# A two-stage convolution block: each engine's program as one free sequence over the images instead of a repeated period

## The chip, the cores and the metric

The kernel runs on one core of a Trainium2 chip. The metric is the device time of one execution in microseconds (us), less is better. Five engines each work through their own queue in order: TensorE (PE in the profile), VectorE (DVE), ScalarE (ACT), GpSimd (POOL) and SyncE (SP), which here only issues DMA transfers. They meet through semaphores.

## The reference

The input x is 8 images of 32 channels, 64 x 64, float32. Two residual blocks follow each other, each behind a group norm with one group per channel:

```python
x = x + L0_conv_ref(gn(x), gate, value, geom, pw weights)   # adaptive 3x3 kernel, R = 4 kernels per pixel
x = x + L1_conv_ref(gn(x), w1, w2, w3)                      # three 3x3 convolutions, 32-64-64-32

# inside L0: per pixel, from 1x1 products of the normed x
mu   = softmax(gate)                                        # 4 weights
kern = exp(-(pu / sig_u) ** 2 - (ps / sig_s) ** 2)          # 4 x 9 taps, from theta, base, hyper
w    = mu * kern; w = w / (sum(w) + 1e-6)
agg  = einsum('brsl,bcsl->brcl', w, patches of the value)   # 4 x 32 channels
out  = einsum('bkhw,ok->bohw', agg, pw_w) + pw_b
```

L1 is three plain 3x3 convolutions in a row.

## The kernel before, in words

**Front of an image (L0).** An image lies in SBUF as 4 quarters of 16 rows by 32 channels on 128 partitions. `gn1_stats`, `gn1_sums`, `gn1_spread`, `gn1_scale`, `gn1_rstd`, `gn1_bias` pass the statistics over VectorE, TensorE and GpSimd; `norm1` (ScalarE) writes the normed xc. `geometry` (L386) makes the gate and geometry values of all pixels, and the eight parts of `tap_weights` on VectorE and six on ScalarE turn them into five tap weights per pixel: the centre and four pairs, since opposite taps have the same weight. `v_product` (L395) and `v_evict` make the value image vn, `halo` copies its border rows between quarters by DMA, and `pair_sum` (L1019, GpSimd) adds opposite neighbours. For each of 10 units u (two halves h of five taps) `values` (L412) transposes the value onto pixels, and `mult` (L712, VectorE, 2,048 elements per partition) multiplies it with the weights. `add_products` (L1003 on GpSimd, L722 on VectorE) adds the five products of a half; in image 0 three of the four adds of a half are done by TensorE in the transposes. `transpose_sums` (L427) transposes back, `sums_out` copies to SBUF, `pointwise` (L440) is the 1x1 product, `residual` (L741) adds x and the bias into x2.

**Between.** The second norm (`gn2_...`, `norm2`) writes y, which is split into a high and a low part (`split_high` on ScalarE L924, `split_low` on VectorE L755). `by_slots` (L287) moves both by DMA into the layout of the convolutions, four groups of 4 high and 4 low transfers each. `by_quads` (L296) moves x2 to x2r, for the last add.

**Convolutions (L1).** Eleven chunks of output rows: four of layer 1, five of layer 2, two of layer 3. A term (`conv_term`, L366) is three matmuls, high by high, low by high, high by low weight. There are 60 terms per image: chunks of layer 1 have 3 each, of layer 2 6, of layer 3 9. `high_part` (ScalarE L929) rounds a chunk, `take_high` (L380) subtracts it in PSUM, `low_part` (ScalarE L937, for the last image VectorE L730) copies the rest. Two PSUM banks alternate, so a chunk starts only when the chunk two before it has its low part out. `result` (L763, VectorE) adds the last two chunks to x2r, and `store` writes them.

**Order.** Every engine has a `body(i)`, a list of steps with image offsets written out by hand; `run_images` calls it for i from -4 to 12, and `on` drops steps of images that don't exist:

```python
def on(i, step, *args):
    if 0 <= i < IMAGES:
        step(i, *args)
...
convs(i - 3, 57, 58)
on(i - 1, transpose_sums, 1)
```

So each engine repeats one period per image. TensorE has the convolutions of image i - 2 between the front steps of images i - 1 and i. In the first periods the conv steps are empty, in the last ones the front steps are.

Of the kernel before, what the change touches and what calls it, by code (L numbers as in the profile page):

```python
# [26 lines left out]
FIRST, LAST = -4, IMAGES + 5  # L27
# [35 lines left out]


def conv_l0_l1_kernel(nc, x, geo_w, geo_bias, val_w, pw_t, pw_b, w1, w2, w3, ident, sel_quarter,
                      masks, consts, out):
    ctx = ExitStack()
    with ctx:
# [110 lines left out]

        def on(i, step, *args):  # L180
            if 0 <= i < IMAGES:
                step(i, *args)

        def run_images(body):
            for i in range(FIRST, LAST):
                body(i)
# [61 lines left out]
        def _(sp):  # L248
# [56 lines left out]
            def body(i):  # L305
                on(i - 1, by_slots, 0, False)
                on(i - 1, by_slots, 1, False)
                on(i - 1, by_slots, 0, True)
                on(i - 1, by_slots, 1, True)
                on(i - 1, by_slots, 2, False)  # L310
                on(i - 1, by_slots, 2, True)
                on(i - 1, by_slots, 3, False)
                on(i - 1, by_slots, 3, True)
                on(i + 1, halo)
                on(i - 2, store)
                on(i - 1, by_quads)
                on(i + 2, load_x)

            run_images(body)
# [21 lines left out]
        def _(pe):  # L341
# [127 lines left out]
            def convs(i, first, end):  # L469
                for k in range(first, end):  # L470
                    on(i, conv_term, k)

            def body(i):
                convs(i - 3, 41, 42)
                on(i - 1, values, 4)
                convs(i - 3, 42, 46)
                on(i - 1, values, 5)
                on(i, geometry)
                convs(i - 3, 46, 48)
                on(i - 3, take_high, 8)  # L480
                convs(i - 3, 48, 50)
                on(i, v_product, 0)
                convs(i - 3, 50, 51)
                on(i - 1, values, 6)
                on(i - 1, values, 7)
                convs(i - 3, 51, 55)
                on(i, v_product, 1)
                convs(i - 3, 55, 57)
                on(i - 1, transpose_sums, 0)
                convs(i - 3, 57, 58)  # L490
                on(i - 1, transpose_sums, 1)
                on(i - 1, transpose_sums, 2)
                convs(i - 3, 58, 60)
                convs(i - 2, 0, 3)
                on(i - 1, transpose_sums, 3)
                on(i - 1, values, 8)
                convs(i - 2, 3, 4)
                on(i - 2, take_high, 0)
                convs(i - 2, 4, 6)
                on(i - 1, values, 9)  # L500
                convs(i - 2, 6, 7)
                on(i - 2, take_high, 1)
                convs(i - 2, 7, 12)
                on(i - 2, take_high, 2)
                on(i - 1, pointwise, 0)
                convs(i - 2, 12, 13)
                on(i - 2, take_high, 3)
                convs(i - 2, 13, 18)
                on(i - 1, transpose_sums, 4)
                on(i - 1, transpose_sums, 5)  # L510
                convs(i - 2, 18, 19)
                on(i - 1, transpose_sums, 6)
                on(i - 2, take_high, 4)
                on(i - 1, transpose_sums, 7)
                convs(i - 2, 19, 20)
                on(i, values, 0)
                convs(i - 2, 20, 21)
                on(i - 1, pointwise, 1)
                convs(i - 2, 21, 26)
                on(i, values, 1)  # L520
                convs(i - 2, 26, 27)
                on(i - 1, gn2_sums, 0)
                convs(i - 2, 27, 29)
                on(i - 1, gn2_sums, 1)
                on(i - 2, take_high, 5)
                on(i, values, 2)
                convs(i - 2, 29, 30)
                on(i + 1, gn1_sums, 0)
                convs(i - 2, 30, 31)
                on(i - 2, take_high, 6)  # L530
                on(i + 1, gn1_sums, 1)
                convs(i - 2, 31, 40)
                on(i - 2, take_high, 7)
                on(i, values, 3)
                convs(i - 2, 40, 41)

            run_images(body)

        @block.vector
        def _(dve):  # L540
# [225 lines left out]
            def body(i):  # L766
                on(i - 4, mult, 7)
                on(i - 4, mult, 8)
                on(i - 4, add_products, 1, 1)
                on(i - 4, mult, 9)  # L770
                on(i - 5, low_part, 0)
                on(i - 4, add_products, 1, 2)
                on(i - 3, tap_weights, 4)
                on(i - 4, add_products, 1, 3)
                on(i - 3, tap_weights, 5)
                on(i - 4, residual, 0)
                on(i - 3, split_weights)
                on(i - 3, tap_weights, 6)
                on(i - 3, tap_weights, 7)
                on(i - 4, residual, 1)  # L780
                on(i - 4, gn2_stats, 0)
                on(i - 5, low_part, 1)
                on(i - 4, gn2_stats, 1)
                on(i - 3, mult, 0)
                on(i - 4, gn2_spread)
                on(i - 2, gn1_stats)
                on(i - 4, gn2_scale)
                on(i - 2, gn1_spread)
                on(i - 5, low_part, 2)
# [38 lines left out]
        def _(act):  # L828
# [111 lines left out]
            def body(i):  # L940
# [163 lines left out]
```

## Time and profile before

| | us |
|---|---|
| median of 3 runs | 549.23 |
| lowest, highest | 548.38, 549.37 |
| the profiled execution | 549.03 |
| its span | 547.2 |
| TensorE busy (mean granted clock 0.973) | 483.3 |
| VectorE busy | 419.4 |
| ScalarE busy | 216.3 |
| GpSimd busy | 191.4 |

Times inside the span count from its start. The span is what the profiler saw of the engines; the execution is 1.8 us longer. "Busy" of TensorE counts a matmul from its start to its modelled end, and matmuls overlap, so a busy share of 100% does not say that each matmul takes its shortest time. The granted clock is a share of the full TensorE clock: 1.00 is 2.4 GHz, 0.50 is 1.2 GHz. A line such as "[2.67 <-DVE prod L722]" says that the engine had been idle for 2.67 us and that the event which ended it came from VectorE's instruction of line 722.

### The profile page before, as it was taken

What the parts mean: (1) busy time and instruction counts of PE and PEld (TensorE: products, weight loads), DVE (VectorE), ACT (ScalarE), POOL (GpSimd) and SP (SyncE); (2) the same over time, 40 slices, a digit from 0 to 9 for tenths busy, and PEclk for the clock granted to TensorE, in tenths of its full rate; (3) what the DMA queues carried; (4) which work ended last, traced back from release to release, by engine and by line L of the source; (5) the groups of instructions that cost most, each with busy time, mean ns of one, the idle gap of its engine ahead of it and who ended that gap; (6) DMA issues with size and microseconds to landing.
All of it is one profiled execution on the core that took longest, in us unless ns stands there. A gap on an engine that the chain in (4) does not pass through costs nothing.

```text
span 547.2 us, 7160 instructions
## 1 busy us (share of the span) xinstructions
PE 483.3 (88%) x2527; PEld 391.8 (72%) x2527; DVE 419.4 (77%) x553; ACT 216.3 (40%) x408; POOL 191.4 (35%) x95
## 2 busy tenths in 40 slices
PE   2505973789999999999999999999999999998995
PEld 2204752566887788777977797779777987886894
DVE  2598678999898989898989989998989698412211
ACT  1520631265335543643355344644364313340110
POOL 1305524572366117520934083506370542000000
PEclk9999995589999999999999999999999999999999
DMA  4100002430144113421233124321431144024302
GB/s 145 42 1 0 5 0 56 98 72 17 46 97 100 40 38 87 93 59 44 69 95 69 47 53 107 65 55 41 100 77 25 36 95 86 22 56 107 70 5 38
DMA packets 40275, 32.23 MB, mean 59 GB/s; under 512 B 26160, under 2 KB 30768, under 8 KB 40240
## 3 DMA queue, kind: packets, MB, share of 16 engines
q1 hardware_dynamic: 40240, 31.78, 25.1%
q8 instruction: 20, 0.33, 0.3%
q14 instruction: 15, 0.12, 0.1%
HBM read 5.66 MB, written 4.19 MB: 18 GB/s over the span
## 4 chain that ended last, share of the span: by engine, by line
PE 64%; DVE 16%; issue 9%; SPq 4%; ACT 2%; POOL 1%; DMA 1%; DVEq 0%; ACTq 0%; POOLq 0%
PE conv_ps L366 42%; PE agg_ps L427 7%; DVE prod L712 6%; DVE prod L722 5%; PE val_ps L412 5%; SPq L287 4%; PE geo_ps L395 3%; PE geo_ps L386 3%; PE pw_ps L440 2%; PE conv_ps L380 2%; DMA xraw<-in_x 1%; POOL prod L1003 1%; DVE st L546 1%; DVE trig L643 1%; POOL vs L1019 1%
## 5 line engine op out<-in xcount | busy, mean ns | idle before, releaser
L712 DVE TENSOR_TENSOR prod<-val_ps,tapw 128x2048 f32<-128x2048 f32 x80 | 181.0, 2284 | 11.6 <-PE val_ps L412 10.2
L366 PE MATMUL conv_ps<-c_hi,wc_hi 128*128 128x448 f32 (+2 forms) x384 | 157.1, 409 | 0.0
L366 PE MATMUL conv_ps<-c_hi,wc_lo 128*128 128x448 f32 (+2 forms) x384 | 144.6, 376 | 0.0
L366 PE MATMUL conv_ps<-c_lo,wc_hi 128*128 128x448 f32 (+2 forms) x384 | 144.1, 375 | 0.0
L1003 POOL TENSOR_TENSOR prod<-prod 128x2048 f32<-128x2048 f32 x23 | 112.5, 4894 | 16.4 <-DVE prod L712 16.4
L1019 POOL TENSOR_TENSOR vs<-vn 128x1024 f32<-128x1024 f32 x32 | 69.6, 2185 | 74.2 <-ACT vn L843 73.4
L722 DVE TENSOR_TENSOR prod<-prod 128x2048 f32<-128x2048 f32 x35 | 88.7, 2533 | 1.0 <-POOL prod L1003 0.5
L366 PEld LDWEIGHTS conv_ps<-c_hi,wc_hi 128*128 128x128 f32 x384 | 72.5, 189 | 21.7 <-issue 8.3
L366 PEld LDWEIGHTS conv_ps<-c_hi,wc_lo 128*128 128x128 f32 x384 | 72.3, 188 | 10.6
L366 PEld LDWEIGHTS conv_ps<-c_lo,wc_hi 128*128 128x128 f32 x384 | 72.7, 189 | 9.7 <-issue 2.4
L929 ACT ACTIVATE c_hi<-conv_ps 128x512 fp32r<-128x512 f32 (+4 forms) x88 | 41.9, 485 | 86.4 <-PE conv_ps L366 86.2
L412 PE MATMUL val_ps<-ident_sb,vs 128*128 128x128 f32 x256 | 42.3, 300 | 24.0 <-DVE prod L712 22.2
L937 ACT ACTIVATE c_lo<-conv_ps 128x512 fp32r<-128x512 f32 (+4 forms) x77 | 36.3, 481 | 68.1 <-PE conv_ps L380 67.8
L993 POOL TENSOR_TENSOR gn<-gn 128x1 f32<-128x1 f32 x8 | 4.4, 552 | 167.7 <-DVE gn L560 167.7
L412 PEld LDWEIGHTS val_ps<-ident_sb,vs 128*128 128x128 f32 x256 | 34.4, 155 | 32.2 <-DVE prod L712 23.6
L427 PE MATMUL agg_ps<-ident_sb,prod 128*128 128x128 f32 x352 | 47.0, 278 | 7.6 <-DVE prod L722 5.9
L427 PEld LDWEIGHTS agg_ps<-ident_sb,prod 128*128 128x128 f32 x352 | 41.5, 144 | 16.6 <-issue 9.9
L908 ACT ACTIVATE agg<-agg_ps 128x512 f32<-128x512 f32 x64 | 36.5, 593 | 25.5 <-PE agg_ps L427 25.4
L366 PE MATMUL conv_ps<-xq_hi,wc_hi 128*128 128x512 f32 x96 | 40.1, 418 | 1.6 <-DMA xq_lo<-y_lo 1.6
L763 DVE TENSOR_TENSOR x2r<-conv_ps,x2r 128x512 f32<-128x512 f32 x16 | 11.0, 688 | 36.1 <-PE conv_ps L366 36.1
L366 PE MATMUL conv_ps<-xq_lo,wc_hi 128*128 128x512 f32 x96 | 38.6, 402 | 0.0
L366 PE MATMUL conv_ps<-xq_hi,wc_lo 128*128 128x512 f32 x96 | 38.4, 400 | 0.0
(107 smaller groups left out, 506.6 us busy)
## 6 DMA issues: line engine op xcount, KB each, us to landing
xq_hi<-y_hi SPq DMA_DIRECT2D x128, 66.0 KB, 2.0
xq_lo<-y_lo SPq DMA_DIRECT2D x128, 66.0 KB, 2.0
xraw<-in_x SPq DMA_DIRECT2D x32, 128.0 KB, 2.8
x2r<-x SPq DMA_DIRECT2D x128, 32.0 KB, 1.9
out_y<-x2r SPq DMA_DIRECT2D x32, 128.0 KB, 2.8
prod<-in_w SPq DMA_DIRECT2D x1, 576.0 KB, 4.8
vn<-vn SPq DMA_DIRECT2D x16, 24.8 KB, 1.8
prod<-in_w SPq DMA_DIRECT2D x1, 384.0 KB, 3.9
```

Of the source, the lines that this page charges most:

```text
L287: sp.dma_start(dst[C * s:C * s + C, j0:j0 + K8, :].bitcast(F32), src[C * g:C * g + C, (s + 1) % 2, :, :].bitcast(F32)).then_inc(xq_in[g], 16)
L366: mm = nc.tensor.matmul(bank[:, 0:conv_cols(n)], weights, lo if part == 1 else hi, start=term == part == 0, stop=final and part == 2)
L386: mm = nc.tensor.matmul(geo_ps[:, k * GEO:(k + 1) * GEO], xc[:, k * P:(k + 1) * P], geo_w_sb[:, :], start=k == 0, stop=k == K8 - 1, skip_g ...
L412: mm = nc.tensor.matmul(val_ps[u % 2][:, kk * P:(kk + 1) * P], src, ident_sb[:, :], is_transpose=True, start=kk == 0, stop=kk == KK - 1, s ...
L427: mm = nc.tensor.matmul(agg_ps[n % 2][:, kk * P:(kk + 1) * P], product(i, TAPS * h + b)[:, at0:at0 + P], ident_sb[:, :], is_transpose=True ...
L712: v.tensor_tensor(dst, val.unsqueeze(2).to_broadcast([P, B, R, C]), wgt.unsqueeze(3).to_broadcast([P, B, R, C]), ALU.mult).then_inc(mult_d ...
L722: v.tensor_tensor(product(i, TAPS * h + a), product(i, TAPS * h + a), product(i, TAPS * h + b), ALU.add).then_inc(add_v, 1)
L908: s.activation(agg[:, n % G, :], agg_ps[n % 2][:, :], ACT.Copy).then_inc(agg_sb, 1)
L929: op = s.activation(hi, src, ACT.Copy)
L937: op = s.activation(lo, src, ACT.Copy)
L1003: p.tensor_tensor(product(i, TAPS * h + a), product(i, TAPS * h + a), product(i, TAPS * h + b), ALU.add).then_inc(add_g, 1)
L1019: p.tensor_tensor(vs[:, n], vn[:, a[0], a[1]], vn[:, b[0], b[1]], ALU.add).then_inc(pairs_done, 1)
```

## The change

`on`, `run_images` and the five `body` functions go. In their place each engine has a flat list of calls, one per step and image. The steps' own code, their waits, buffers and engines are unchanged, and each engine issues the same instructions. Only their order in each queue is new, and it is no longer the same for every image. From the diff (removed lines are all of this kind: `on(i - 3, mult, 1)`):

```diff
-FIRST, LAST = -4, IMAGES + 5
-        def run_images(body):
-            for i in range(FIRST, LAST):
-                body(i)
@@ SyncE
-            def body(i): ...
+            load_x(0); load_x(1); halo(0); halo(1); load_x(2)
+            by_slots(0, 0, False) ... by_slots(0, 3, True)
+            halo(2); by_quads(0); load_x(3)
...
+            by_slots(2, 2, True); halo(4); by_slots(2, 3, False); by_slots(2, 3, True)
+            store(1); by_quads(2); load_x(5)
...
+            store(4); halo(7); by_quads(5)
@@ TensorE
+            gn1_sums(0, 0); gn1_sums(0, 1); geometry(0); v_product(0, 0); v_product(0, 1)
+            gn1_sums(1, 0); gn1_sums(1, 1)
+            values(0, 0) ... values(0, 4); geometry(1); values(0, 5)
+            transpose_sums(0, 0); transpose_sums(0, 1); values(0, 6); transpose_sums(0, 2)
+            values(0, 7); v_product(1, 0); transpose_sums(0, 3); v_product(1, 1)
+            values(0, 8); values(0, 9); values(1, 0); pointwise(0, 0)
+            transpose_sums(0, 4) ... transpose_sums(0, 7); pointwise(0, 1)
+            gn2_sums(0, 0); values(1, 1); gn2_sums(0, 1); gn1_sums(2, 0)
+            values(1, 2); values(1, 3); gn1_sums(2, 1); values(1, 4); values(1, 5)
+            geometry(2); values(1, 6); values(1, 7); convs(0, 0, 1); v_product(2, 0)
+            convs(0, 1, 3); v_product(2, 1); convs(0, 3, 6); transpose_sums(1, 0)
...
+            convs(0, 53, 60); transpose_sums(2, 0); transpose_sums(2, 1); convs(1, 0, 1)
...
+            convs(1, 53, 60); convs(2, 0, 1); transpose_sums(3, 0)
...
+            convs(2, 55, 57); transpose_sums(4, 0)        # then (5, 0) behind convs(3, 56, 58),
+            # (6, 0) behind convs(5, 0, 2), (7, 0) behind convs(5, 49, 58)
...
+            pointwise(7, 1); convs(6, 22, 26); gn2_sums(7, 0); convs(6, 26, 27)
+            take_high(6, 5); gn2_sums(7, 1); convs(6, 27, 34) ... convs(7, 0, 60)
@@ VectorE
+            gn1_stats(0); gn1_spread(0); gn1_scale(0); gn1_bias(0)
+            tap_weights(0, 0); tap_weights(0, 1); split_weights(0)
+            tap_weights(0, 2); tap_weights(0, 3); gn1_stats(1); tap_weights(0, 4); tap_weights(0, 5)
+            gn1_spread(1); tap_weights(0, 6); gn1_scale(1); tap_weights(0, 7); gn1_bias(1)
+            mult(0, 0) ... mult(0, 4); tap_weights(1, 0); tap_weights(1, 1); mult(0, 5)
+            tap_weights(1, 2); mult(0, 6); tap_weights(1, 3); mult(0, 7); mult(0, 8); mult(0, 9)
+            residual(0, 0); tap_weights(1, 4); gn2_stats(0, 0); tap_weights(1, 5); tap_weights(1, 6)
+            residual(0, 1); gn2_stats(0, 1); gn2_spread(0); tap_weights(1, 7); gn2_scale(0)
+            mult(1, 0); gn1_stats(2); gn2_bias(0); gn1_spread(2); mult(1, 1); mult(1, 2); mult(1, 3)
+            gn1_scale(2); split_low(0); gn1_bias(2); mult(1, 4); mult(1, 5)
...
+            mult(3, 5); tap_weights(4, 2); result(1, 0); add_products(3, 0, 3)
+            tap_weights(4, 3); mult(3, 6); result(1, 1)
...
+            tap_weights(7, 2); result(4, 0); add_products(6, 0, 3); tap_weights(7, 3); result(4, 1)
@@ ScalarE
+            norm1(0); split_weights(0); tap_weights(0, 0); v_evict(0, 0)
...
+            high_part(6, 5); low_part(6, 5); norm2(7); split_high(7); high_part(6, 6)
@@ GpSimd
+            gn1_rstd(0); pair_sum(0, 0); pair_sum(0, 1); gn1_rstd(1); pair_sum(0, 2); pair_sum(0, 3)
+            add_products(0, 0, 0); add_products(0, 1, 0); pair_sum(1, 0)
```

In the diff each call stands on a line of its own; here they are joined, and "..." between two calls of one kind means the ones in between.

## Rows read from the trace of the kernel before

**Rows 1.** The page: busy time by engine, and TensorE's busy tenths in 40 slices

```profile
PE 483.3 (88%) x2527; PEld 391.8 (72%) x2527; DVE 419.4 (77%) x553; ACT 216.3 (40%) x408; POOL 191.4 (35%) x95
PE   2505973789999999999999999999999999998995
```

**Rows 2.** The span in stretches: length, busy us of each engine, clock, DMA

```profile
core 0: us, PE busy (x) PEld busy (x) DVE busy (x) ACT busy (x) POOL busy (x), PEclk, DMA share, GB/s
84.00:108.00 24.00, 14.44 (x51) 11.05 (x52) 22.17 (x32) 6.28 (x10) 13.02 (x5) 0.51 0.32 80
108.00:115.00 7.00, 4.33 (x17) 3.15 (x16) 6.96 (x7) 3.57 (x9) 2.96 (x1) 0.75 0.45 106
163.00:219.00 56.00, 55.53 (x303) 45.43 (x302) 51.15 (x67) 26.41 (x52) 24.14 (x9) 1.00 0.29 67
111.50:478.60 367.10, 363.39 (x1956) 296.02 (x1957) 327.49 (x399) 168.61 (x323) 150.41 (x54) 1.00 0.28 64
```

**Rows 3.** The chain that ended last, in order of time: start, us, what

```profile
137.43 3.37 PE conv_ps L366 x15
...
170.95 3.63 PE conv_ps L366 x15
...
421.38 3.37 PE conv_ps L366 x15
```

**Rows 4.** VectorE's waits, 163 to 219.7 us: total, times, longest; first two of five

```profile
DVE x2r L763 <- PE conv_ps L366: 1.6, 1, 1.6
DVE prod L712 <- PE val_ps L412: 1.0, 1, 1.0
```

**Rows 5.** TensorE's timeline in a period: start, us, line, operation, idle before

```profile
188.69 1.06 PE L427 MATMUL agg_ps<-ident_sb,prod 128*128 128x128 f32 x8 [0.47 <-DVE prod L722]
```

**Rows 6.** TensorE's timeline, 98 to 115 us

```profile
98.67 3.67 PE L386 MATMUL geo_ps<-geo_w_sb,xc 128*128 128x64 f32 x16 [0.28 <-ACT xc L836]
...
111.46 2.83 PE L427 MATMUL agg_ps<-ident_sb,prod 128*128 128x128 f32 x12 [2.67 <-DVE prod L722]
113.95 0.78 PE L366 MATMUL conv_ps<-xq_hi,wc_hi 128*128 128x512 f32 x1
```

**Rows 7.** SyncE's DMA issues at the start; third, of the page: KB, us to landing

```profile
6.35 1.38 SPq L266 DMA_DIRECT2D prod<-in_w  x3
...
98.84 4.94 SPq L287 DMA_DIRECT2D xq_lo<-y_lo  x8
...
prod<-in_w SPq DMA_DIRECT2D x1, 576.0 KB, 4.8
```

**Rows 8.** Timelines of VectorE and GpSimd, 24 to 83 us

```profile
24.20 4.36 POOL L1019 TENSOR_TENSOR vs<-vn 128x1024 f32<-128x1024 f32 x2 [0.82 <-DMA vn<-vn]
24.62 2.08 DVE L642 TENSOR_TENSOR trig<-trig 128x128 f32<-128x128 f32 x1 [3.79 <-ACT trig L886]
...
31.61 2.56 DVE L686 TENSOR_TENSOR wc_lo<-prod,wc_hi 128x2304 fp32r<-128x2304 f32 x1
...
37.31 2.29 DVE L712 TENSOR_TENSOR prod<-val_ps,tapw 128x2048 f32<-128x2048 f32 x1
...
43.02 6.68 DVE L712 TENSOR_TENSOR prod<-val_ps,tapw 128x2048 f32<-128x2048 f32 x3
...
68.25 4.49 DVE L712 TENSOR_TENSOR prod<-val_ps,tapw 128x2048 f32<-128x2048 f32 x2 [2.87 <-PE val_ps L412]
72.66 0.28 DVE L642 TENSOR_TENSOR trig<-trig 128x128 f32<-128x128 f32 x1
...
81.82 0.88 DVE L741 SCALAR_TENSOR_TENSOR x<-pw_ps,pw_b_sb,xraw 128x256 f32<-128x256 f32 x2 [0.93 <-PE pw_ps L440]
```

**Rows 9.** Timelines of VectorE and TensorE, 471 to 507 us

```profile
471.17 0.88 DVE L741 SCALAR_TENSOR_TENSOR x<-pw_ps,pw_b_sb,xraw 128x256 f32<-128x256 f32 x2 [4.03 <-DMA x2r<-x]
...
478.60 0.28 PE L466 MATMUL pw_ps<-gn,sel_sb 128*128 128x1 f32 x2
...
506.07 0.48 PE L366 MATMUL conv_ps<-xq_hi,wc_hi 128*128 128x512 f32 x1 [1.62 <-DMA xq_lo<-y_lo]
```

More of the change, by code:

```diff
@@ L470, in convs @@
                 for k in range(first, end):
[L471 to L535, printed above, removed]
@@ L539, in _ @@
+            convs(6, 39, 44)
+            take_high(6, 8)
+            convs(6, 44, 60)
+            convs(7, 0, 60)
         @block.vector
@@ new lines, in _ @@
+            tap_weights(1, 5)
+            tap_weights(1, 6)
+            residual(0, 1)
+            gn2_stats(0, 1)
+            gn2_spread(0)
+            tap_weights(1, 7)
+            gn2_scale(0)
+            mult(1, 0)
+            gn1_stats(2)
+            gn2_bias(0)
+            gn1_spread(2)
+            mult(1, 1)
+            mult(1, 2)
+            mult(1, 3)
+            gn1_scale(2)
+            split_low(0)
+            gn1_bias(2)
+            mult(1, 4)
+            mult(1, 5)
@@ new lines, in _ @@
+            residual(1, 1)
+            gn2_stats(1, 0)
+            gn2_stats(1, 1)
+            tap_weights(2, 7)
+            mult(2, 0)
+            gn2_spread(1)
+            gn1_stats(3)
+            gn2_scale(1)
+            mult(2, 1)
+            gn1_spread(3)
+            gn2_bias(1)
+            mult(2, 2)
+            mult(2, 3)
+            gn1_scale(3)
+            split_low(1)
+            gn1_bias(3)
+            mult(2, 4)
+            mult(2, 5)
+            tap_weights(3, 0)
@@ new lines, in _ @@
+            tap_weights(3, 6)
+            residual(2, 1)
+            gn2_stats(2, 0)
+            gn2_stats(2, 1)
+            tap_weights(3, 7)
+            mult(3, 0)
+            gn2_spread(2)
+            gn1_stats(4)
+            gn2_scale(2)
+            mult(3, 1)
+            gn1_spread(4)
+            gn2_bias(2)
+            mult(3, 2)
+            gn1_scale(4)
+            mult(3, 3)
+            split_low(2)
+            gn1_bias(4)
+            mult(3, 4)
+            tap_weights(4, 0)
@@ new lines, in _ @@
+            residual(3, 0)
+            tap_weights(4, 6)
+            residual(3, 1)
+            gn2_stats(3, 0)
+            gn2_stats(3, 1)
+            tap_weights(4, 7)
+            gn2_spread(3)
+            gn2_scale(3)
+            mult(4, 0)
+            gn1_stats(5)
+            gn2_bias(3)
+            gn1_spread(5)
+            mult(4, 1)
+            mult(4, 2)
+            mult(4, 3)
+            gn1_scale(5)
+            split_low(3)
+            gn1_bias(5)
+            mult(4, 4)
@@ new lines, in _ @@
+            tap_weights(5, 5)
+            residual(4, 0)
+            tap_weights(5, 6)
+            residual(4, 1)
+            gn2_stats(4, 0)
+            gn2_stats(4, 1)
+            tap_weights(5, 7)
+            mult(5, 0)
+            gn2_spread(4)
+            gn1_stats(6)
+            gn2_scale(4)
+            gn1_spread(6)
+            gn2_bias(4)
+            gn1_scale(6)
+            mult(5, 1)
+            gn1_bias(6)
+            mult(5, 2)
+            mult(5, 3)
+            split_low(4)
@@ new lines, in _ @@
+            tap_weights(6, 5)
+            residual(5, 0)
+            tap_weights(6, 6)
+            gn2_stats(5, 0)
+            residual(5, 1)
+            gn2_stats(5, 1)
+            tap_weights(6, 7)
+            gn2_spread(5)
+            gn2_scale(5)
+            mult(6, 0)
+            gn1_stats(7)
+            gn2_bias(5)
+            gn1_spread(7)
+            mult(6, 1)
+            gn1_scale(7)
+            mult(6, 2)
+            mult(6, 3)
+            split_low(5)
+            gn1_bias(7)
@@ L983, in _ @@
+            high_part(7, 7)
+            high_part(7, 8)
         @block.gpsimd
```

1200 lines of the change are left out of this document (1078 added, 122 removed).

## The prediction

> **What bounds the kernel now.** I read the busy shares first, then the span in stretches, then the chain, then each engine's timeline at the start, in one period and at the end. An image is named by its number, a step by its function: `values(0, 6)` is unit 6 of image 0.
>
> TensorE has the largest share (88%), VectorE is next (77%), and TensorE's slices read 9 from the tenth to the 36th, where the first nine are thin [rows 1]. From 163 to 219 us TensorE is busy 55.53 of 56 us and VectorE 51.15; from 111.5 to 478.6 us TensorE is busy 363.39 of 367.1 us, which leaves 3.7 us of idle time, and VectorE has 39.6 us [rows 2]. Busy need not mean working, so I looked at the pace in the chain: 15 conv matmuls of 512 columns take 3.63 us, 15 of 448 columns 3.37 [rows 3], so a term of the convolutions (three matmuls) takes 0.72 or 0.67 us, and nothing in a period runs slower than that. The same conv step comes back after (421.38 - 137.43) / 5 = 56.8 us [rows 3]. VectorE has five waits in a period, 4.0 us in all, the longest 1.6 us for the last conv chunk [rows 4]; TensorE has one, 0.47 us for an add [rows 5]. So the middle is bound by TensorE's own instructions, with VectorE 4 us behind it. The change keeps all of them. A new order cannot make the middle much shorter: 3.7 us is all that is idle there.
>
> What can be gained lies ahead of 111.5 us, where TensorE is idle or at half clock, and in how much conv work is done by then. From 84 to 108 us it is busy 14.44 of 24 us at a granted clock of 0.51 [rows 2], and the first conv matmul starts at 113.95 us, behind three groups of transposes that wait 2.67 us for an add [rows 6], although its input was asked for by 103.8 us (98.84 + 4.94) [rows 7].
>
> **The start, step by step.** VectorE leads the chain from 31 to 111 us, so I follow it.
>
> (a) Up to `mult(0, 0)`. Before, it begins at 37.31 us. Three things change. `split_weights` (2.56 us) no longer stands behind tap weight part 5 but ahead of part 2: its weights land about 12.5 us (issued by 7.7 us, 4.8 us to landing [rows 7]), ScalarE converts them while it waits for geometry, so this costs some 0.9 us down the table-load chain and saves 1.9 us later (0.7 of the 2.56 covered the wait for an exponential). The two trig adds take 2.08 us each while GpSimd runs two pair sums of 4.36 us together, and 0.28 us at 72.66 us with GpSimd idle [rows 8]. In the new order GpSimd stops for `gn1_rstd(1)` after `pair_sum(0, 1)`, so only one pair sum is in their way: 1.7 us less. `gn1_stats(1)` and the small steps of image 1 move into gaps here (an idle wait of 3.79 us [rows 8]); its x is now loaded at once. Sum: 0.9 - 1.9 - 1.7 + 0.2 = 2.5 us earlier, `mult(0, 0)` at 34.8.
>
> The Trainium skill (SBUF — State Buffer, "SBUF: two separate sides") says that a VectorE instruction with two SBUF inputs and a GpSimd one that reads SBUF lock each other out for a whole instruction. By it the 1.7 us are certain; were the 2.08 us due to something else, (a) would give 0.8 instead.
>
> (b) The multiplications of image 0. Between `mult(0, 0)` and `mult(0, 1)` the old order holds the norm of image 1, from 39.60 to 43.02 us [rows 8]: gone, 3.4 us. A wait of 0.5 us before `mult(0, 4)` goes too. A third one of 2.87 us, until 68.25 [rows 8], comes from `values` standing behind four transposes; the new order puts `values(0, 6)` and `(0, 7)` between them: 2.7 us. So image 0's last product ends at 68.25 + 4.49 = 72.7, less 2.5, 3.4, 0.5 and 2.7 = 63.6 us, 9.1 earlier. Transposes and pointwise stay on the path (81.82 - 72.7 = 9.1 us [rows 8]), and `residual(0, 1)` comes at 72.7 instead of 81.82.
>
> (c) From there to the first transposes of image 1, 29.6 us before (81.82 to 111.46). Two edits cost here: `tap_weights(1, 7)` now stands behind `residual` (1.0 us), and `split_low(0)` (1.5 us) ahead of `gn1_bias(2)`, so `geometry(2)`, 3.67 us at half clock [rows 6], starts later. Two gain, 0.7 us of small waits and 0.6 us behind the load of x. The adds of image 1 end at 103.3, 7.9 us earlier, and the conv terms put in front of the transposes make it 104.5: **7.0 us**.
>
> (d) Conv terms. y of image 0 is split 8.8 us earlier; 8 high and 8 low transfers of 5 us each (4.94 the low ones) follow [rows 7], so chunk 0 can start about 97 us and chunk 1 at 102. The new order puts terms 0 to 5 ahead of `transpose_sums(1, 0)`, where TensorE idled; the old one has none. At the other end `gn2_sums(7, 1)` stands behind term 26 of image 6, before behind term 28. Between the two points TensorE has 8 terms less: 6 x 0.72 + 2 x 0.67 = **5.7 us**.
>
> (e) Clock. The 12 transposes at 111.46 take 2.83 us [rows 6] where 8 take 1.06 at full clock [rows 5], so some 1.4 too much, and the first conv matmul takes 0.78, for which and for the next I count 0.5 too much, since the clock is at the lower of its levels for most of 108 to 115 us [rows 2, 6]. With geometry, conv and v products close behind each other from 91.5 us I expect the full level by 104: **1.9 us**; bounds 0 (it stays low) and 3 (also geometry speeds up).
>
> (f) The middle. The new order is uneven: there are 54 terms between the first transposes of images 1 and 2, then 61, 56, 61, 64, 56, where the old order had 57 and then 60 each. The first is the tight one: 54 terms are about 51.5 us of TensorE, the old period less 3 terms and the extra start, and VectorE needs 51.15 us of work plus its round trips. I take **2.5 us lost**, 0.4 us a period on top of the 0.47 us that was idle [rows 5]. Bounds: 3.7 gained (all idle time gone), 10 lost (1.6 us a period, the wait of VectorE for a conv chunk, in all six).
>
> (g) The end. From `gn2_sums(7, 1)` at 478.60 a fixed line runs over the norm, y and 16 + 8 + 8 transfer issues to the conv chunk that starts at 506.07 after 1.62 us of waiting, and then 41.1 us of conv work [rows 9]. Its steps keep their order, less one small ScalarE copy (0.5 us). TensorE's backlog grows by 1.3 us and fills that wait. So the end moves with (c) to (f); 0 to 0.5 us more. `residual(7, 0)` also waits 4.03 us for the reload of x2r [rows 9], which hangs on `result(5, 1)`; this moves with TensorE.
>
> (h) Moved halos, stores and loads on the DMA queue: a halo now stands inside the transfers of y. It is read by pair sums that are wanted some 20 us later, so 0; it costs something if the v copy that it waits for comes later than the y before it.
>
> Sum against the profiled execution, 549.03 us (span 547.2; the median 549.23 is 0.2 above): 7.0 + 5.7 + 1.9 - 2.5 = 12.1 us less: **537 us**.
>
> **The rivals.** (1) VectorE becomes the second bound and the start's gain is mostly given back: for it, 51.15 us of work beside a 51.5 us first period; against it, 39.6 us of idle VectorE over the middle. With 1.5 us a period lost, 14.6 - 9 = 5.6: 543.4 us. (2) Everything fits, the middle's idle time goes too: 14.6 + 3.7 + 0.5 = 18.8 us, 530. Against it: first-period tightness. (3) Slower: `result`. VectorE takes its queue in order, and both `result` steps wait for the last conv chunk of an older image. In the period they stand at one fixed place with 1.6 us of waiting; now they move, in images 3 and 6 split around the add of the next sums, so that everything behind them (tap weights, `mult(i, 6)`) stands until convs end. VectorE has 4.0 us a period to give; the point from which it decides is 4.0 + 14.6 / 6 = 6.4 us more, a wait of 8.0 us per image. At 9 us it is (7.4 - 4.0) x 6 - 14.6 = 5.8 us slower, 555. Against it: the conv terms ahead of the adds moved the same way. (4) The order does not matter, since the in-order queues wait for the same semaphores: the start gains nothing, 549. Against it: the 3.4 us of (b) are work of image 1 in front of image 0's path.
>
> The Trainium skill (TensorE: Matmul & The Clock Gate, "What's actually happening") has the clock rise only after sustained activity; by it conv terms strewn into waits before 104 us may leave the clock low, and (e) would give nothing: 539. It agrees with the 0.51 from 84 to 108 us, where TensorE was busy 14.44 of 24 us.
>
> **How the numbers follow.** My forecast with its spread (533 to 541) gets 0.64, rival 1 0.18, rival 2 0.07, rival 3 0.08, rival 4 0.03. The range takes in (f)'s bounds toward rivals 1 and 2: 531 to 546. A measurement tells 0.2%, 1.1 us, from no change. Faster 0.89 (the first three cases), same 0.03, slower 0.08.
>
> **What would show it.** `mult(0, 0)` near 35 us; `residual(0, 1)` near 73; the first conv matmul near 97; the first transposes of image 1 near 104.5; full clock from then on; TensorE idle under 7 us between there and `gn2_sums(7, 1)` at about 465; L763's wait under 3 us per image. A first conv matmul behind 105, or TensorE idle over 10 us in the middle, would make the forecast wrong.

## The result, and the profile after

The new order takes 556.37 us (median of 4 runs, 555.29 to 556.81) where the old one takes 548.81 (548.25 to 549.37) beside it: ratio 1.0135 [1.0114, 1.0155], 7.6 us slower. The prediction was 537 us with a range of 531 to 546, so it has the wrong sign. The profiled execution has a span of 554.2 us, 7.0 more than before. Line numbers are new: `mult` L1159, the add on VectorE L1169, the add on GpSimd L1945, tap weight part 3 L1085 and L1086, `residual` L1188, `result` L1210, conv L437, transposes L498.

The page, to be read beside [rows 1]: busy time, and TensorE's busy and clock tenths in 40 slices.

```profile
PE 486.4 (88%) x2527; PEld 395.5 (71%) x2527; DVE 434.7 (78%) x553; ACT 216.9 (39%) x408; POOL 192.7 (35%) x95
...
PE   3339655979999889999979999999999999999995
...
PEclk9999875897999999999998999999999999999999
```

The operations are the same, but VectorE is busy 15.3 us longer (434.7 against 419.4). From the tenth slice on TensorE's slices show two 8s and a 7 where [rows 1] has 9s, and the granted clock is down in the tenth slice and in the 22nd. The windows of [rows 2] in the new kernel, and two more behind the largest waits:

```profile
core 0: us, PE busy (x) PEld busy (x) DVE busy (x) ACT busy (x) POOL busy (x), PEclk, DMA share, GB/s
84.00:108.00 24.00, 18.02 (x74) 14.05 (x75) 22.10 (x26) 8.96 (x15) 13.18 (x4) 0.64 0.36 85
108.00:115.00 7.00, 6.30 (x37) 4.87 (x35) 7.00 (x5) 3.62 (x8) 6.47 (x3) 1.00 0.24 55
163.00:219.00 56.00, 50.92 (x276) 40.95 (x276) 52.88 (x62) 23.30 (x42) 25.05 (x9) 1.00 0.25 56
111.50:478.60 367.10, 351.76 (x1867) 286.18 (x1866) 332.46 (x387) 162.90 (x312) 147.23 (x53) 0.98 0.27 62
...
126.00:133.00 7.00, 7.00 (x34) 5.76 (x34) 4.43 (x13) 2.91 (x5) 0.00 (x0) 0.58 0.00 1
...
290.20:297.00 6.80, 6.80 (x23) 5.66 (x24) 5.27 (x5) 4.39 (x8) 3.57 (x2) 0.60 0.47 81
```

The start did what was forecast of it: from 84 to 108 us TensorE has 3.6 us more work, and the clock is 1.00 from 108 to 115 us, before 0.75 [rows 2]. The middle did not. In the same 367.1 us TensorE now idles 15.3 us where it idled 3.7. The old period had one wait of 0.47 us [rows 5]. TensorE's timeline in the new kernel, the first transposes of image 1 and every wait over 1 us from there to 478.6 us:

```profile
107.03 0.63 PE L498 MATMUL agg_ps<-ident_sb,prod 128*128 128x128 f32 x4
...
125.91 1.94 PE L498 MATMUL agg_ps<-ident_sb,prod 128*128 128x128 f32 x8 [4.25 <-DVE prod L1169]
187.30 1.07 PE L498 MATMUL agg_ps<-ident_sb,prod 128*128 128x128 f32 x8 [2.14 <-DVE prod L1169]
207.06 0.38 PE L526 MATMUL geo_ps<-gn,sel_sb 128*128 128x1 f32 x2 [1.61 <-DVE gn L1002]
290.13 0.80 PE L437 MATMUL conv_ps<-xq_hi,wc_hi 128*128 128x512 f32 x1 [3.37 <-DVE x2r L1210]
```

All four are for VectorE. Behind the two longest, the granted clock was 0.58 for 7 us and 0.60 for 6.8 us, that is mostly the lower of the two levels (1.2 GHz); behind the wait of 2.14 us it stayed at 1.00 (187 to 195 us). Which VectorE work became longer, its groups by line show (busy us and mean ns of one behind the bar):

```profile
L1086 DVE TENSOR_TENSOR ch<-ch,geo 128x128 f32<-128x128 f32 x8 | 13.2, 1649 | 0.0
L1085 DVE TENSOR_TENSOR ch<-ch,geo 128x128 f32<-128x128 f32 x8 | 5.9, 738 | 0.5 <-ACT geo L1573 0.5
L1210 DVE TENSOR_TENSOR x2r<-conv_ps,x2r 128x512 f32<-128x512 f32 x16 | 10.8, 683 | 29.1 <-PE conv_ps L437 29.1
```

and the same groups of the kernel before:

```profile
L639 DVE TENSOR_TENSOR ch<-ch,geo 128x128 f32<-128x128 f32 x8 | 2.3, 285 | 0.0
L638 DVE TENSOR_TENSOR ch<-ch,geo 128x128 f32<-128x128 f32 x8 | 4.0, 498 | 0.9 <-ACT geo L878 0.9
L763 DVE TENSOR_TENSOR x2r<-conv_ps,x2r 128x512 f32<-128x512 f32 x16 | 11.0, 688 | 36.1 <-PE conv_ps L366 36.1
```

One small subtract of tap weight part 3 went from 2.3 to 13.2 us in eight instances. (The add L1085 ahead of it grew less, 4.0 to 5.9 us; three of its eight are held up, the longest takes 1.98.) A mean hides how: five of the subtracts take 0.28 us, three take 4.64 (55.01 us), 2.49 (113.73) and 4.65 (284.83). The last one, on VectorE's and GpSimd's timelines, just ahead of the wait of 3.37 us:

```profile
282.43 2.28 DVE L1159 TENSOR_TENSOR prod<-val_ps,tapw 128x2048 f32<-128x2048 f32 x1
...
284.63 0.28 DVE L1085 TENSOR_TENSOR ch<-ch,geo 128x128 f32<-128x128 f32 x1
284.79 4.54 POOL L1945 TENSOR_TENSOR prod<-prod 128x2048 f32<-128x2048 f32 x1 [0.53 <-DVE prod L1159]
284.83 4.65 DVE L1086 TENSOR_TENSOR ch<-ch,geo 128x128 f32<-128x128 f32 x1
...
289.40 1.27 DVE L1210 TENSOR_TENSOR x2r<-conv_ps,x2r 128x512 f32<-128x512 f32 x2
```

`mult(4, 6)` releases GpSimd's 4.54 us add. The new order puts tap weight part 3 of image 5 right behind that `mult`, so its second subtract begins 0.04 us after the add and ends with it. `result` stands behind it, TensorE's next chunk behind `result`. At 55.01 the same happens behind `mult(0, 6)`; at 113.73, behind `mult(1, 8)`, the subtract meets the pair sum that follows GpSimd's add; this is 2.2 of the 4.25 us that TensorE waits behind it. Where such an instruction starts later, it is held for what is left: an L1085 that begins at 164.09, inside a pair sum of 162.29 to 165.92, takes 1.98 us.

**The balance.** From the first transposes of image 1 to `gn2_sums(7, 1)`, and what lies outside (spans of one profiled execution each):

| | us |
|---|---|
| first transposes of image 1, 111.46 [rows 6] to 107.03 | -4.4 |
| low clock behind them, gone: before 0.66 from 111.46 to 116.5, (1 - 0.66) x 5.04 | -1.7 |
| 8 conv terms done ahead or left behind the end | -5.7 |
| TensorE idle, 3.7 to 16.0 | +12.3 |
| low clock behind the two long waits, an estimate from the two windows: 0.42 x 7.0 + 0.40 x 6.8 | +5.7 |
| not accounted for | +1.3 |
| tail from `gn2_sums(7, 1)`, 68.6 [rows 9] to 68.1 | -0.5 |
| sum | +7.0 |

### The profile page after: what moved, and what is told of

Read it like the earlier page. It is cut to its first block, busy times and chain, and to the rows that moved or that the text cites. A ratio compares the mean times of both kernels' runs of the same rounds, so it can differ in the third digit from the quotient of the medians.

```text
span 554.2 us, 7160 instructions
## 1 busy us (share of the span) xinstructions
PE 486.4 (88%) x2527; PEld 395.5 (71%) x2527; DVE 434.7 (78%) x553; ACT 216.9 (39%) x408; POOL 192.7 (35%) x95
## 4 chain that ended last, share of the span: by engine, by line
PE 42%; DVE 23%; issue 19%; POOL 10%; ACT 3%; DMA 1%; SPq 1%; DVEq 0%; POOLq 0%
PE conv_ps L437 30%; DVE prod L1159 11%; POOL prod L1945 8%; DVE prod L1169 5%; PE agg_ps L498 4%; PE val_ps L483 2%; PE pw_ps L511 2%; POOL vs L1961 2%; DMA prod<-in_w 1%; PE geo_ps L457 1%; PE conv_ps L451 1%; POOL gn L1931 1%; PE geo_ps L466 1%; DVE trig L1089 1%; DVE x2r L1210 1%
## 5 line engine op out<-in xcount | busy, mean ns | idle before, releaser
L1159 DVE TENSOR_TENSOR prod<-val_ps,tapw 128x2048 f32<-128x2048 f32 x80 | 180.6, 2282 | 6.2 <-PE val_ps L483 5.0
L437 PE MATMUL conv_ps<-c_hi,wc_hi 128*128 128x448 f32 (+2 forms) x384 | 154.4, 402 | 0.0
L437 PE MATMUL conv_ps<-c_hi,wc_lo 128*128 128x448 f32 (+2 forms) x384 | 144.8, 377 | 0.0
L437 PE MATMUL conv_ps<-c_lo,wc_hi 128*128 128x448 f32 (+2 forms) x384 | 144.5, 376 | 0.0
L1945 POOL TENSOR_TENSOR prod<-prod 128x2048 f32<-128x2048 f32 x23 | 108.1, 4701 | 42.1 <-DVE prod L1159 42.1
L1961 POOL TENSOR_TENSOR vs<-vn 128x1024 f32<-128x1024 f32 x32 | 71.4, 2241 | 66.1 <-ACT vn L1538 57.0
L437 PEld LDWEIGHTS conv_ps<-c_hi,wc_hi 128*128 128x128 f32 x384 | 72.8, 190 | 15.8 <-issue 7.5
L1169 DVE TENSOR_TENSOR prod<-prod 128x2048 f32<-128x2048 f32 x35 | 80.0, 2287 | 1.8 <-POOL prod L1945 0.2
L437 PEld LDWEIGHTS conv_ps<-c_hi,wc_lo 128*128 128x128 f32 x384 | 72.5, 189 | 10.6
L437 PEld LDWEIGHTS conv_ps<-c_lo,wc_hi 128*128 128x128 f32 x384 | 72.9, 190 | 9.8 <-issue 1.7
L498 PE MATMUL agg_ps<-ident_sb,prod 128*128 128x128 f32 x352 | 49.9, 288 | 8.3 <-DVE prod L1169 7.7
L498 PEld LDWEIGHTS agg_ps<-ident_sb,prod 128*128 128x128 f32 x352 | 43.8, 150 | 18.1 <-issue 11.8
L483 PE MATMUL val_ps<-ident_sb,vs 128*128 128x128 f32 x256 | 43.8, 301 | 13.0 <-DVE prod L1159 13.0
L437 PE MATMUL conv_ps<-xq_hi,wc_hi 128*128 128x512 f32 x96 | 42.8, 446 | 4.0 <-DVE x2r L1210 3.8
L437 PE MATMUL conv_ps<-xq_lo,wc_hi 128*128 128x512 f32 x96 | 39.4, 410 | 0.0
L437 PE MATMUL conv_ps<-xq_hi,wc_lo 128*128 128x512 f32 x96 | 39.1, 408 | 0.0
L1210 DVE TENSOR_TENSOR x2r<-conv_ps,x2r 128x512 f32<-128x512 f32 x16 | 10.8, 683 | 29.1 <-PE conv_ps L437 29.1
```

The lines of the kernel that those rows point to most:

```text
L437: mm = nc.tensor.matmul(bank[:, 0:conv_cols(n)], weights, lo if part == 1 else hi, start=term == part == 0, stop=final and part == 2)
L483: mm = nc.tensor.matmul(val_ps[u % 2][:, kk * P:(kk + 1) * P], src, ident_sb[:, :], is_transpose=True, start=kk == 0, stop=kk == KK - 1, s ...
L498: mm = nc.tensor.matmul(agg_ps[n % 2][:, kk * P:(kk + 1) * P], product(i, TAPS * h + b)[:, at0:at0 + P], ident_sb[:, :], is_transpose=True ...
L1159: v.tensor_tensor(dst, val.unsqueeze(2).to_broadcast([P, B, R, C]), wgt.unsqueeze(3).to_broadcast([P, B, R, C]), ALU.mult).then_inc(mult_d ...
L1169: v.tensor_tensor(product(i, TAPS * h + a), product(i, TAPS * h + a), product(i, TAPS * h + b), ALU.add).then_inc(add_v, 1)
L1210: v.tensor_tensor(x2r[:, 8 * n:8 * n + 8, :], ps, x2r[:, 8 * n:8 * n + 8, :], ALU.add).then_inc(out_done, 1)
```

## The experiments

**1. Tap weight part 3 of three images moved.** Part 3 (the add L1085 and the subtract L1086) of images 1, 2 and 5 goes ahead of `mult(i, 6)`, and with it ScalarE's `tap_weights(2, 2)`, which feeds it, one place ahead of `sums_out(1, 0)`.

```diff
+            tap_weights(1, 3)
             mult(0, 6)
-            tap_weights(1, 3)
...
+            tap_weights(2, 3)
             mult(1, 6)
             mult(1, 7)
             mult(1, 8)
-            tap_weights(2, 3)
...
+            tap_weights(5, 3)
             mult(4, 6)
-            tap_weights(5, 3)
```

> The changed kernel (556.4 us) with three steps moved back ahead: tap_weights(1, 3), (2, 3) and (5, 3) on VectorE stand before mult(0, 6), mult(1, 6) and mult(4, 6) instead of behind mult(0, 6), mult(1, 8) and mult(4, 6) (tap_weights(2, 2) on ScalarE moves one place up with it). Theory A, lockout: a 0.28 us subtract with two SBUF inputs that starts together with GpSimd's add waits for all of it (4.64, 2.49 and 4.65 us in the trace of after), so VectorE saves 4.4 + 2.4 + 4.4 = 11 us in three places, TensorE's waits of 4.25 us at 126 and 3.37 us at 290 shrink below 2 us and the lower clock behind each (some 3.4 us each) goes: 541 to 549 us. Theory B, the moved conv terms and result steps: TensorE waits because its own order puts terms too early, and tap weights do not matter: 555 to 557 us.

546.37 us, ratio to before 0.9954 [0.9938, 0.997]: 10.0 us less than the changed kernel. All eight L1086 take 280 ns:

```profile
L1086 DVE TENSOR_TENSOR ch<-ch,geo 128x128 f32<-128x128 f32 x8 | 2.2, 280 | 0.0
```

The three stretched subtracts had 10.9 us in excess of 0.28 (4.36 + 2.21 + 4.37). That the gain is as large is in part chance: VectorE's busy time falls by 3.5 us only (434.7 to 431.2), because other instructions with two SBUF operands now meet GpSimd (2.12 us at 64.26, 1.98 at 275.83, 1.52 at 283.53, 2.48 at 284.98). What counts is where they stand. Of the 9.5 us that the span is shorter, 4.0 lie ahead of the first transposes of image 1 (103.03 for 107.03) and 5.2 between them and `gn2_sums(7, 1)` (373.9 us for 379.1). There TensorE idles 14.2 us instead of 16.0, the wait of 3.37 us for `result` is gone, the longest is 2.80 us at 107.14, and only behind that is the clock down (0.79 from 107 to 115 us). The six instructions of these three steps, out of 7,160, turn the change from slower to slightly faster.

**2. The kernel before with the collision in every period.** The only edit is part 3 behind `mult(i, 6)`, seven times.

```diff
+            tap_weights(i + 1, 3)    # now behind mult(i, 6)
```

> The kernel before (549.2 us) with one part of the change alone: tap_weights(i + 1, 3) stands behind mult(i, 6) instead of in front, in all seven images that have it. Theory A, lockout: the second subtract takes about 4.6 us instead of 0.28 in each, VectorE's later add meets GpSimd less (3.6 back to 2.3 us), so 3 us a period on VectorE, of which 4.0 us of idle time hide most in the middle but nothing in the first period; TensorE's 0.47 us wait grows: 551 to 562 us. Theory B, order of terms: the step is 0.5 us long and its place is free, 549 us within 0.5.

576.96 us, ratio 1.0511 [1.049, 1.0531], 28 us slower, beyond the 551 to 562 expected. Period 3 on the timelines of VectorE, GpSimd and TensorE:

```profile
237.89 4.58 POOL L1946 TENSOR_TENSOR prod<-prod 128x2048 f32<-128x2048 f32 x1
238.00 4.62 DVE L1087 TENSOR_TENSOR ch<-ch,geo 128x128 f32<-128x128 f32 x1
...
242.55 1.27 DVE L1211 TENSOR_TENSOR x2r<-conv_ps,x2r 128x512 f32<-128x512 f32 x2
...
243.28 0.80 PE L437 MATMUL conv_ps<-xq_hi,wc_hi 128*128 128x512 f32 x1 [3.04 <-DVE x2r L1211]
```

All seven are stretched (group mean 4,090 ns over eight). TensorE waits 3.05 us at this place in each of five periods, and the clock from 107 to 479 us is 0.96 where it was 0.99, which the expected range left out. It is slower although VectorE's own adds, six of which are stretched in the kernel before (4.41 us at 120.29), all take 2.28 us here. Of the 27.3 us that the span is longer, 2.4 lie ahead of the first transposes of image 1 (113.86). From there to `gn2_sums(7, 1)` (506.55) TensorE idles 20.6 us, 16.9 more than before, and a clock of 0.97 over these 393 us is an estimated 10 us more. The fall is not the same behind equal waits: behind the one of 3.05 us at 183.38 the clock was 1.00 (183.4 to 190 us), behind the one at 243.28 it was 0.76 (243.3 to 250).

**3. The same order, one operand from PSUM.** As 2, but the two instructions of part 3 read their second operand from PSUM. What lies there by then is the value product of the image, and a wait for its last `v_evict` is added. So this kernel leaves the logarithm of the base out of the tap weights: it is good for its times, not for its output.

```diff
-did(13, v.tensor_tensor(w[:, 0, :], spl[:, 1, :], lb, ALU.add))
-did(14, v.tensor_tensor(w[:, 1, :], spl[:, 1, :], lb, ALU.subtract))
+dve.wait_ge(vc_out, 2 * i + 2)
+did(13, v.tensor_tensor(w[:, 0, :], spl[:, 1, :], geo_ps[:, 0:NW], ALU.add))
+did(14, v.tensor_tensor(w[:, 1, :], spl[:, 1, :], geo_ps[:, 0:NW], ALU.subtract))
```

> e2 (577.0 us: tap_weights(i + 1, 3) behind mult(i, 6)) with the second operand of its two instructions read from PSUM (geo_ps) in place of SBUF; the logarithm of the base is left out of the tap weights by that. Same number, place, length and engine. Port lockout (only two SBUF inputs collide with GpSimd): both take about 0.3 us, 549 to 551 us. If any VectorE instruction started with GpSimd's add is held, or if the place costs by its waits: 570 to 578 us.

547.3 us (10 runs), ratio 0.9974 [0.9958, 0.999]: 29.7 us less than with both operands in SBUF, and somewhat under the 549 to 551 expected; VectorE's adds take 2.28 us here as in 2, which the range left out. The pair in the same period, both within or at the edge of GpSimd's work:

```profile
223.52 1.90 POOL L1963 TENSOR_TENSOR vs<-vn 128x1024 f32<-128x1024 f32 x1 [8.62 <-ACT vn L1540]
225.03 0.28 DVE L1087 TENSOR_TENSOR ch<-ch,geo_ps 128x128 f32<-128x128 f32 x1
225.22 0.28 DVE L1088 TENSOR_TENSOR ch<-ch,geo_ps 128x128 f32<-128x128 f32 x1
225.37 4.62 POOL L1947 TENSOR_TENSOR prod<-prod 128x2048 f32<-128x2048 f32 x1
```

The first starts inside a pair sum of GpSimd and takes 0.28 us (0.55 in 2); seven of its eight instances start so, and none is longer. Here the subtract is done before the add begins or just as it does. In one period it starts inside the add, 0.03 us behind its start in both kernels; first 3, then 2:

```profile
113.41 4.59 POOL L1947 TENSOR_TENSOR prod<-prod 128x2048 f32<-128x2048 f32 x1 [0.53 <-DVE prod L1161]
113.44 0.28 DVE L1088 TENSOR_TENSOR ch<-ch,geo_ps 128x128 f32<-128x128 f32 x1
```

```profile
115.89 4.58 POOL L1946 TENSOR_TENSOR prod<-prod 128x2048 f32<-128x2048 f32 x1 [0.52 <-DVE prod L1160]
115.92 4.69 DVE L1087 TENSOR_TENSOR ch<-ch,geo 128x128 f32<-128x128 f32 x1
```

So neither the place, nor the queue, nor GpSimd's semaphore made the cost of 2, but the second SBUF operand. The Trainium skill says that a VectorE instruction with two SBUF inputs and a GpSimd one that reads SBUF block each other for a whole instruction (SBUF — State Buffer, "SBUF: two separate sides"). These runs agree, with 4.69 us for a 0.28 us instruction that starts inside a 4.58 us add.

**4. Conv terms moved up.** Terms 18 to 21 of image 0 ahead of the transposes that wait 4.25 us at 125.91.

```diff
+            convs(0, 18, 22)
             transpose_sums(1, 4)
...
-            convs(0, 18, 19)
+            convs(0, 22, 23)
...
-            convs(0, 19, 20)
+            convs(0, 23, 24)
...
-            convs(0, 20, 25)
+            convs(0, 24, 25)
```

> The changed kernel with four conv terms (18 to 21 of image 0) ahead of transpose_sums(1, 4) instead of behind, where TensorE waits 4.25 us for VectorE's add. Theory A and my reading that the six early terms of step (d) were only moved from one wait to another: TensorE fills 2.5 us of that wait, and the clock does not fall behind it (3.4 us): 550 to 553 us. Theory C, the wait is hidden, since VectorE bounds the next images too: 555 to 557 us.

556.97 us, ratio 1.0133 [1.0104, 1.0162], as the changed kernel's 1.0135. The wait of 4.25 us has become one of 3.02 us under another name, and the others stayed:

```profile
125.01 0.48 PE L437 MATMUL conv_ps<-c_hi,wc_hi 128*128 128x448 f32 x1 [3.02 <-ACT c_lo L1633]
...
292.00 0.50 PE L437 MATMUL conv_ps<-xq_hi,wc_hi 128*128 128x512 f32 x1 [3.37 <-DVE x2r L1211]
```

The terms need a low part of ScalarE. It stands in its queue behind the square of tap weight part 4, which waits for VectorE:

```profile
123.84 0.63 ACT L1588 ACTIVATE trig<-trig 128x512 f32<-128x512 f32 x1 [2.85 <-DVE trig L1091]
124.38 0.58 ACT L1633 ACTIVATE c_lo<-conv_ps 128x512 fp32r<-128x512 f32 x1
```

So the moved terms hung on VectorE's chain as well, by way of ScalarE. A miss for the idea that strewing terms differently mends this gap; it does not test what the terms would bring if they were free to start.

**5 and 6. The new start alone.** The changed kernel's order up to `residual(0, 1)`, the old order behind it. The sixth kernel moves one more step:

```diff
+            tap_weights(1, 3)
             mult(0, 6)
-            tap_weights(1, 3)
```

> The changed kernel's order up to pointwise(0, 1), residual(0, 1), sums_out(0, 7) and pair_sum(1, 2), and the order of before behind them. residual(0, 1) ended at 76.8 us in after and at 82.7 in before. Theory A and D (the start gained, the middle lost): the start's 5 to 6 us are kept, because the period's order behind it has none of the collisions: 542 to 545 us. Theory E (what the start gains is lost anyway, as VectorE is late in image 1): 548 to 550 us.

> e4 (543.4 us: the new start, the old order behind it) with tap_weights(1, 3) ahead of mult(0, 6). In the trace of e4 its second subtract still takes 4.64 us at 54.57, against GpSimd's add. Lockout: VectorE leads there, so the start gets 4.2 us shorter less about 0.5 for waiting on ScalarE's logarithm: 539 to 540.5 us. If the start is bound by TensorE's transposes instead: 543 us.

543.38 us, ratio 0.9899 [0.9879, 0.9918], and 538.78 us, 0.9817 [0.9792, 0.9841]; the latter again, on another chip: 538.39, 0.981 [0.9791, 0.9829]. The one subtract at 55 us is worth 4.6 us, and the whole start 10 us. The first transposes of image 1, of the fifth and of the sixth:

```profile
105.37 2.89 PE L498 MATMUL agg_ps<-ident_sb,prod 128*128 128x128 f32 x12 [3.09 <-DVE prod L1170]
```

```profile
101.06 2.89 PE L498 MATMUL agg_ps<-ident_sb,prod 128*128 128x128 f32 x12 [2.81 <-DVE prod L1170]
```

In the old middle TensorE idles 3.3 and 4.4 us from 107 to 479 us, against 16.1 in the changed kernel. The step at 55 us is moved in experiment 1 too, where it brings 4.0 of the 10.0 us.

**7. The changed middle, cleaned further.** As 1, with the norm steps of images 3 and 4 ahead of `mult(i, 1)` and tap weight part 4 of four images behind `add_products(i, 1, 2)`, ScalarE's part 4 with it.

```diff
+            gn1_spread(3)
             mult(2, 1)
-            gn1_spread(3)
...
+            tap_weights(3, 4)    # behind add_products(2, 1, 2); also images 5, 6, 7
```

> e1 (546.4 us: the changed kernel with part 3 ahead of mult) and the other collisions seen in its trace taken out too: gn1_spread(3) and (4) ahead of mult(i, 1) (3.97 us at 196), tap_weights 4 of images 3, 5, 6, 7 behind add_products(i, 1, 2) as in the old period (1.5 + 2.5, 1.5 + 2.5, 0.5 + 2.5 us), ScalarE's part with it. Lockout: 3.7 + some 9 us less on VectorE, of which the middle had 4 us a period to hide; TensorE's waits at 180, 200 and 299 us (2.16, 1.62, 1.44) go: 540 to 544 us. If what is left is the unevenness of the term counts: 546 us.

542.74 us, ratio 0.9906 [0.9873, 0.994]: another 3.6 us. The places moved in 1 and 7 are worth some 14 us together (10.0 + 3.6). To the sixth kernel 4 us are left. They are not a matter of how much VectorE is held up: its stretched instructions have 11.3 us in excess here and 14.1 in the sixth kernel. From its first transposes of image 1 (102.45) to `gn2_sums(7, 1)` (471.95) TensorE still idles 10.5 us; in the sixth kernel it idles 4.4 us between the same two steps.

**8 and 9. Early conv terms on a clean start.** The sixth kernel with terms 0 to 2 of image 0 ahead of `transpose_sums(1, 0)` and up to four terms more ahead of the steps behind; the ninth also has ScalarE's `high_part(0, 0)` ahead of `tap_weights(2, 3)`.

```diff
+            convs(0, 0, 2)
             v_product(2, 1)
+            convs(0, 2, 3)
             transpose_sums(1, 0)
             transpose_sums(1, 1)
             transpose_sums(1, 2)
-            convs(0, 0, 3)
+            convs(0, 3, 4)
...
-            convs(0, 13, 18)
+            convs(0, 13, 22)
             transpose_sums(1, 4)
```

> e5 with conv terms 0 to 2 of image 0 ahead of transpose_sums(1, 0), where TensorE waits 3.1 us, and the front steps of image 1 up to gn1_sums(3, 1) 2 to 4 terms later than in the old order, the old order from term 36. Step (d) of the prediction, with what it lacked: if VectorE's 4 us of idle time in the next period takes up the later front steps, the terms stay gained: 1.5 to 3 us under e5, 536.5 to 538.5. If VectorE bounds the second image too, the same as e5: 539 to 540.5.

In the eighth, the wait went to a high part that stands in ScalarE's queue behind tap weights:

```profile
108.33 0.47 PE L451 MATMUL conv_ps<-c_hi,neg_i 128*128 128x512 f32 x1 [2.94 <-ACT c_hi L1626]
```

> As the kernel with conv terms 0 to 2 of image 0 ahead of transpose_sums(1, 0) (540.6 us), with ScalarE's high_part(0, 0) ahead of tap_weights(2, 3), whose two table loads of 1.28 us held the first conv term back. Theory A (a conv term taken into a wait is a gain once nothing queues in front of it): its last wait of 2.94 us for high_part goes, 536 to 538 us. Theory B (VectorE's chain from the start on sets the time, and TensorE waits for it with or without those terms done): 539 to 541 us, and the wait comes back before a later group of transposes.

> The same kernel as e5_start_clean, again, beside the one with early terms: 538 to 540 us by both theories; it gives the size of what two chips' runs differ by.

540.6 us, 0.9849 [0.982, 0.9877], and 540.1 us (537.65 to 541.91), 0.9836 [0.9812, 0.986], against 0.981 [0.9791, 0.9829] of the sixth kernel beside the ninth: no gain. In the windows, first of the ninth, then of the sixth kernel run beside it:

```profile
84.00:107.00 23.00, 18.98 (x79) 14.49 (x79) 22.83 (x25) 10.35 (x20) 14.15 (x4) 0.66 0.41 97
107.00:480.00 373.00, 367.63 (x1974) 299.33 (x1975) 321.91 (x398) 168.27 (x324) 146.00 (x54) 1.00 0.28 63
```

```profile
84.00:107.00 23.00, 16.57 (x57) 12.68 (x58) 22.83 (x24) 9.83 (x19) 13.52 (x4) 0.58 0.40 94
107.00:480.00 373.00, 369.65 (x1992) 301.26 (x1991) 322.20 (x399) 169.25 (x325) 147.48 (x54) 1.00 0.28 63
```

The early terms give TensorE 2.4 us more work ahead of 107 us, and it idles 2.0 us more behind. The profiled spans differ by 0.9 us the other way than the medians (535.9 and 536.8), so whether the terms give 1 us or cost 1 stays open. The 2.2 us (3 x 0.72) that step (d) would count for them would put the ninth at 0.981 - 0.004 = 0.977, outside its interval.

## Why the prediction was wrong

**The failed step is (f), the middle.** It forecast 2.5 us lost, at most 10; measured are 12.3 us of idle TensorE and, behind the two longest waits, 5.7 us of low clock. Its own sign of being wrong, TensorE idle over 10 us in the middle, came true with 16.0. (The bound of 10 us lost gives 549.0 - 14.6 + 10 = 544.4; the range went to 546, and even so 556.4 is far outside.) I had looked at the number of conv terms between transposes, and treated tap weight steps between two `mult`s as movable at their own length. In (a) I had used [rows 8]: the trig add of 2.08 us beside GpSimd's pair sums, and 0.28 without, and named the reason. I did not ask the same question at the places to which the change moves two-operand SBUF work in the middle. The question is: which GpSimd instruction does the `mult` ahead of it release? Experiment 1 shows that three such places cost 10.0 us, 2 that the place alone makes the old order slow too, 3 that the second SBUF operand is the cause, 7 that the smaller places cost 3.6 us.

These places are not the whole of it. From the first transposes of image 1 to `gn2_sums(7, 1)` the kernel before takes 367.2 us, and (d), (e) and (f) put the new one at 367.2 - 5.7 - 1.9 + 2.5 = 362.1. Measured are 379.1, 17 us more. Experiment 1 brings it to 373.9 and 7 to 369.5: 9.6 of the 17 us. The other 7.4 stay with these places mended. TensorE's idle time accounts for 4.3 of them (10.5 us, where 3.7 + 2.5 were forecast), and of the rest no run shows the cause.

**(a), (b), (c): right but for the same mistake.** `mult(0, 0)` starts at 35.27 (34.8 forecast), the first conv matmul at 99.97 (97). `residual(0, 1)` at 76.05 (72.7) and the first transposes at 107.03 (104.5): the subtract at 55.01 took 4.64 us there. Without it they are at 72.04 and 103.03 in the first experiment. The sixth kernel, with the new start and the old middle, gains 10.0 to 10.5 us, and all of it lies ahead of the first transposes of image 1 (101.06 for 111.46). (a) to (c) had promised 7.9 for it without conv terms in front. The gain of (e) is not in it: behind these transposes the clock is 0.68 for 5 us, as it was 0.66 before.

**(d), conv terms, 5.7 us: not a gain of its own.** TensorE had them done, and idled more instead: the seventh kernel, which has the 8 terms, idles 6.1 us more between the same two steps than the sixth, which has none (10.5 against 4.4). Experiments 8 and 9 show that three terms on a clean start bring no gain that can be measured. In 4 the four moved terms could not start earlier. Work taken ahead on the bound engine counts only if the next wait does not end at the same time as before; the longest waits hang on VectorE's chain. In the sum it should have been set against (f), not added.

**(e), clock: right at its place, 1.7 us for the 1.9 forecast**. The 1.9 itself was a little high: 12 transposes at the pace of [rows 5] take 1.59 us, so 2.83 are 1.2 too much and not 1.4. Not foreseen was that waits in the middle would bring the clock down again: 5.7 us behind the waits of 4.25 and 3.37 us. So a long wait can be dearer than its length, but not every time (experiment 2). The Trainium skill (TensorE: Matmul & The Clock Gate, "What's actually happening") has the clock set by how busy TensorE has been of late. The two windows at 0.58 and 0.60 agree; the 1.00 behind 3.05 us of waiting in experiment 2 says that the length of one wait alone does not settle it.

**(g), (h): right.** The tail is 0.5 us shorter (forecast 0 to 0.5); no halo shows among TensorE's or VectorE's long waits.

**The rivals.** Rival 3 (slower, 555 us) has nearly the number, 556.4, but by luck, since its mechanism did not occur: VectorE's waits at `result` fell from 36.1 to 29.1 us, they did not grow. It was the reverse, TensorE waiting 3.37 us for `result`, since VectorE came to it late. Rival 1 (VectorE becomes a bound, 543.4) has the right engine, but it priced VectorE's amount of work at 9 us of the start's gain. The changed kernel lost more than the whole gain, to instructions that were held up; with three of these places mended the first experiment still measures 546.4. Rival 4 is refuted by the fifth and sixth kernels: the order of the start alone is worth up to 10 us.

**Not settled:** 1.3 us of the balance, and why the cleaned new order (542.7) stays behind the sixth kernel (538.8). 1.4 us of that are the later first transposes (102.45 for 101.06), 1.5 the middle (369.5 for 368.0 us) although it has 8 terms less; the uneven number of terms per period is the candidate, not shown.

The best version is the sixth kernel, 538.4 to 538.8 us, 10 us below the kernel before and 18 below the changed one.

## What to carry to other kernels

When an instruction is moved, look at what the other engines will be doing at its new place, above all at the instruction ahead of it: what that one releases starts at the same moment. Here a VectorE instruction with two SBUF operands was cheap ahead of the one that releases GpSimd, or with one operand read from PSUM. And look at minimum and maximum of each group, not its mean: a 0.28 us line that is sometimes 4.65 us says that the price belongs to the place. Nor is the sum of such prices the gain to expect: in experiment 1 others appeared elsewhere, at places that cost less.

## What the runs showed of the hardware that was not expected

A 0.28 us VectorE subtract took as long as the whole GpSimd add that started 0.04 to 0.11 us ahead of it (4.65 beside 4.54, 4.62 beside 4.58). A `mult` of 2,048 elements with one operand in PSUM keeps 2.29 us beside the same add, and `result` its 0.69. Even an instruction of one element per partition is held: `gn1_spread` L1002 took 3.95 us at 203.05 for 0.22 elsewhere, and TensorE's wait of 1.61 us at 207.06 follows from it. And seven such subtracts, 32.4 us of VectorE time for 2.0, cost 28 us of 549, although TensorE is the engine that is busy 88% of the time. That this is nearly their whole length is chance: VectorE's busy time grew by 22.0 us only (441.4 for 419.4), as its adds were no longer held up, and an estimated 10 us are TensorE's lower clock.
